# A software-pipelined Perceiver layer: key steps moved a period ahead, the shared unit moved behind the tiles

## What is computed

```python
x = x + xattn(layernorm(x), ctx)     # 16 heads of 128, q and k RMS-normed per head; softmax over 257; @ Wo
x = x + attn(layernorm(x))           # 16 heads of 16, 4 kv heads, rotary, causal; ternary weights; rms_norm(y) @ Wproj
x = x + ffn(layernorm(x))            # below

probs = softmax(xt @ Wg); eidx = argmax(probs); gate = probs[eidx]     # 2048 tokens, 8 experts, top 1
pos = cumsum(onehot) - 1; keep = pos < 256                             # capacity 256 per expert
out = gate * keep * (silu(xe @ W1[e]) * (xe @ W3[e])) @ W2[e]          # hidden width 352
shared = (silu(xt @ sw1) * (xt @ sw3)) @ sw2                           # every token
return out + shared
```

## Time and profile before

| | |
|---|---|
| median of 3 runs | 1421.3 us (1420.99 to 1423.54) |
| the profiled execution | 1421.9 us, its span 1420.0 |
| mean granted TensorE clock | 0.963 |
| busy, share of the span: PE / DVE / ACT / POOL | 89% / 64% / 62% / 40% |
| instructions | 34911 |
| chain that ended last: PE / DVE / issue / ACT / POOL | 51% / 17% / 10% / 8% / 4% |

### The profile page before, as it was taken

How to read it: one execution, slowest core, us unless ns; L and a number is a source line. 1 busy time by engine, 2 the same in 40 slices (tenths; PEclk the granted TensorE clock), 3 DMA queues, 4 the chain that set the end, 5 groups by cost and what they waited for, 6 DMA issues and landing times.

```text
span 1420.0 us, 34911 instructions
## 1 busy us (share of the span) xinstructions
PE 1268.5 (89%) x10526; PEld 852.0 (60%) x10526; DVE 913.5 (64%) x3312; ACT 886.6 (62%) x3732; POOL 571.5 (40%) x1371
## 2 busy tenths in 40 slices
PE   5877999999999999999999999999999999983596
PEld 2644666666665656566666666665656566661485
DVE  6754767767676767676767767776767676753132
ACT  5455676757585767767676767585767767651132
POOL 1053262625344352525262625344352525244153
PEclk9988999999999999999999999999999999995799
DMA  9020010101010000000010101010000000210251
GB/s 351 16 84 8 13 36 11 34 11 34 8 34 11 24 22 23 22 13 25 11 34 11 34 11 34 12 31 11 25 21 23 22 15 23 111 33 2 72 191 47
DMA packets 36563, 55.18 MB, mean 39 GB/s; under 512 B 6797, under 2 KB 29482, under 8 KB 35601
## 3 DMA queue, kind: packets, MB, share of 16 engines
q1 hardware_dynamic: 32064, 46.53, 10.5%
q0 software_dynamic: 3376, 7.98, 1.7%
q10 hardware_dynamic: 1056, 0.02, 0.0%
HBM read 46.54 MB, written 8.42 MB: 39 GB/s over the span
## 4 chain that ended last, share of the span: by engine, by line
PE 51%; DVE 17%; issue 10%; ACT 8%; POOL 4%; DMA 1%; POOLq 0%; DVEq 0%; ACTq 0%
PE AB L600 27%; PE Db L600 9%; PE Eb L600 7%; DVE kst L1374 3%; PE C L600 3%; DVE rq L1431 2%; PE C L729 2%; PE C L744 2%; POOL prob L1190 2%; ACT prob L1022 2%; ACT AB L954 2%; DVE pT L1563 1%; DVE px L1645 1%; ACT wt_q L946 1%; ACT pxT L1054 1%
## 5 line engine op out<-in xcount | busy, mean ns | idle before, releaser
L954 ACT ACTIVATE AB<-AB 128x128 f32<-128x128 f32 (+1 forms) x1160 | 303.4, 262 | 95.8 <-PE AB L600 92.6
L1145 POOL TENSOR_TENSOR pjunk<-pjunk 128x1 f32<-128x1 f32 x289 | 56.3, 195 | 679.3 <-DVE sinv L1558 384.8
L1374 DVE BATCH_NORM_STATS2 kst<-AB 128x6 f32<-128x256 f32 x512 | 181.8, 417 | 107.3 <-PE AB L600 104.7
L600 PE MATMUL AB<-wk_hi,c_hi 128*128 128x512 f16 x512 | 199.5, 390 | 19.3 <-POOL c_lo L1151 7.4
L954 ACT ACTIVATION_READ_ACCUMULATOR AB<-AB 128x1 f32 (+1 forms) x1160 | 216.1, 186 | 0.0
L600 PE MATMUL AB<-wk_lo,c_hi 128*128 128x512 f16 x512 | 198.2, 387 | 0.0
L600 PE MATMUL AB<-wk_hi,c_lo 128*128 128x512 f16 x512 | 197.6, 386 | 0.0
L1022 ACT ACTIVATE prob<-prob,nbias,rq 128x257 f32<-128x257 f32 x256 | 150.6, 591 | 9.2 <-DVE nbias L1553 9.2
L1190 POOL TENSOR_SCALAR prob<-prob,sinv 128x257 f32<-128x257 f32 x256 | 129.2, 505 | 20.1
L600 PE MATMUL AB<-ctxT,qpT 128*128 128x257 f32 x512 | 123.2, 383 | 11.5 <-ACT pxT L1054 11.5
L600 PEld LDWEIGHTS AB<-wk_hi,c_hi 128*128 128x128 f16 x512 | 50.9, 99 | 101.7 <-issue 29.4
(11 more groups left out here) (282 smaller groups left out, 2868.5 us busy)
## 6 DMA issues: line engine op xcount, KB each, us to landing
ctxT<-in_ctxT SPq DMA_DIRECT2D x64, 128.5 KB, 2.1
ctxn<-in_ctxn SPq DMA_DIRECT2D x64, 128.0 KB, 2.1
xin<-in_x SPq DMA_DIRECT2D x16, 128.0 KB, 2.2
prob<-in_wqT SPq DMA_DIRECT2D x1, 2048.0 KB, 16.5
xres<-in_x SPq DMA_DIRECT2D x16, 128.0 KB, 2.1
expert_rows<-base POOLq DMA_DIRECT2D x1, 2048.0 KB, 9.3
out<-base SPq DMA_DIRECT2D x16, 128.0 KB, 1.7
wq_hi<-in_w SPq DMA_DIRECT2D x2, 768.0 KB, 4.2
```

The costliest lines, as they stand in the source:

```text
L600: return pe.matmul(out, lhsT, rhs, start=start, stop=stop)
L954: ins = nc.scalar.activation(k, k, ACT.Square, accum_out=sums[0:m, h:h + 1])
L1145: own.mark(pool.tensor_tensor(pjunk[:, 0:1], pjunk[:, 1:2], pjunk[:, 1:2], ALU.mult))
L1374: ins = V.bn_stats(stats[:, 0, 2 * half + n], AB[0:m, 2 + half, 2 * D * n:2 * D * (n + 1)])
```

## The change

Six things are changed.

1. **Key steps ahead.** A0 to A3 are the key steps of batches 0 and 1 (formerly K0 to K3) of tile i+2, run in period i, one period before the rest of that tile's front half, with their splits a0, a1 (POOL), and AN, gAN, an for the inverse roots. In the prologue they are added at its end, and the loop's period keeps K4 to K7. There are now 14 loop periods, then FIN (tile 14's back half and tile 15's front half, without the A steps), then LAST, both written out as straight code.
2. **Shared unit behind the periods.** up and dn leave the period. SP stores x2 to out and xn2T to a part of the scratch output (store_halfway). LAST does U0 to U15 and D0 to D15 for all 16 tiles with the last tile's own steps among them; SP loads xn2T and x2 back four tiles deep and stores the sums. The rows of the experts are loaded after D9.
3. **Compact last key.** plast is 128 by 12 for a batch, turned by one matmul, and ACT spreads it over the four groups with four scaled copies.
4. **VectorE.** rq is one multiply by a mask, a matmul rx by a spreading matrix, a multiply and a reduction. The four adds of key heads become one, ysq's reduction two adds, and the norm's last operation and the one-hot compare take a broadcast operand in place of a scalar.
5. **Tags.** Each period, POOL sends the tags of the tile before (tg); LAST has two left.
6. **Order.** The lists are written anew. DVE's loop is unrolled by 7.

```diff
-    "PE": """K0 pt3 K1 X K2 o3 K3 f Q xt1 K4 qkv QP rk0 s0 qk sc rk1 K5 K6 K7 pt0 pv s1 st pr rk2 s2 o0 xt2 rk3
-              lg up s3 pt1 dn pos o1 pt2 o2""".split(),
-    "POOL": """h0 n3 h1 X h2 c0 c1 r0 cl ln1 r1 h3 n0 r2 y r3 ln2 c2 n1 c3 n2 scat""".split(),
+    "PE": """pt3 K4 o3 K5 f X rk0 K6 Q xt1 K7 qkv QP rx s0 qk sc rk1 s1 rk2 A0 pt0 pv rk3 s2 st pr s3 A1 pt1 o0 xt2 lg
+              A2 pos o1 pt2 A3 o2""".split(),
+    "ACT": """tl3 ph3 K4 oh3 K5 X K6 Q rk0 xt1 gRQ K7 qkv gqkv gKN1 QP qk e0 rk1 sc rk2 A0 tl0 ph0 pv rk3 e1 e2 A1 tl1
+              ph1 xt2 oh0 e3 lg A2 oh1 tl2 ph2 A3 oh2 gAN""".split(),
+    "DVE": """dp3 K4 do3 K5 X XL f K6 Q RQ K7 qkv KN1 rq qr rx s0 kn1 sc i0 s1 sm A0 dp0 ys yv s2 i1 s3 pr i2 ln2 A1
+              dp1 do0 lg i3 pos A2 do1 dp2 A3 AN an do2""".split(),
+    "POOL": """n3 h2 h3 tg X r0 ln1 r1 c1 c0 c3 r2 a0 n0 a1 r3 c2 cl y n1 ln2 n2 scat""".split(),
+LAST_ORDER = {
+    "PE": """U0 pt3 U1 o3 f D0 U2 xt1 D1 qkv U3 D2 qk sc U4 D3 pv U5 st pr D4 U6 xt2 lg D5 U7 pos D6 U8 D7 U9 D8 U10 D9
+             U11 D10 U12 D11 U13 D12 U14 D13 U15 D14 D15""".split(),
+    "POOL": """n3 tg ln1 y ln2 scat""".split(),
...
+            def store_halfway(p):
+                sp.wait_ge(drained["E"].sem, drained["E"].at(p, "pr"))
+                sp.dma_start(d["out"][bass.ds(p.tile * P, P), :], x2[:]).then_inc(x2_out.sem, 16)
+                sp.wait_ge(drained["D"].sem, drained["D"].at(p, "xt2"))
+                sp.dma_start(turned_rows[bass.ds(p.tile * P, P), :], xn2T[:].rearrange("p k n -> p (k n)")).then_inc(xn2T_out.sem, 16)
...
+            for n in range(TILES):
+                s = BANK_PAIRS[n][1]
+                sp.wait_ge(filled[s].sem, filled[s].at(LAST, f"U{n}"))
+                if n + 4 < TILES - 1:
+                    load_turned(n + 4)
+                sp.wait_ge(drained["E"].sem, drained["E"].at(LAST, f"D{n}"))
+                sp.dma_start(d["out"][n * P:(n + 1) * P, :], back_of(n)).then_inc(sum_out[n % 4] if n < TILES - 1 else last_out, 16)
+                if n + 4 < TILES - 1:
+                    sp.wait_ge(sum_out[n % 4], 16 * (n // 4 + 1))
+                    load_back(n + 4)
+                if n == 9:
+                    load_rows()
...
-                for g in range(G):
-                    ins = mm(Db[0:LK, P * g:P * (g + 1)], plast[:, b, g], ident16[:])
-                ins.then_inc(filled["D"].sem, 1)
+                mm(Db[0:LK, 0:P], plast[:, b], ident16[:]).then_inc(filled["D"].sem, 1)
...
+                for g in range(G):
+                    ins = nc.scalar.activation(pTl[0:LK, b % 2, P * g:P * (g + 1)], Db[0:LK, 0:P], ACT.Copy,
+                                               scale=own_group[0:LK, g:g + 1])
...
+            def step_rx(p):
+                pe.wait_ge(rqt_ready.sem, rqt_ready.at(p, 0))
+                start(p, "rx")
+                mm(Db[:, 0:NB * H], spread32[:], rqm[:].rearrange("p n m -> p (n m)")).then_inc(filled["D"].sem, 1)
...
-                for b in range(NB):
-                    for m in range(4):
-                        src = rqt[SQ * b:SQ * (b + 1)].rearrange("p (g m) -> p g m", m=4)[:, :, m]
-                        ins = V.tensor_scalar(rq[SQ * m:SQ * (m + 1), G * b:G * (b + 1)], src, 1.0 / WQK_SCALE, None, ALU.mult)
...
-                V.tensor_scalar(out, x, mv[:, 0:1], rstd[:, n:n + 1], ALU.subtract, ALU.mult).then_inc(xn_ready.sem, 1)
+                V.scalar_tensor_tensor(out, x, mv[:, 0:1], rstd[:, n:n + 1].broadcast_to([P, DIM]), ALU.subtract, ALU.mult)\
+                    .then_inc(xn_ready.sem, 1)
...
-                    for n in range(TILES - 1):
-                        put_tags(n)
...
-            with loop(pool) as i:
+            with loop(pool) as i:
                 tile(Period("full", i))
+            tile(FIN)
             tile(LAST)
```

More of the change, by code:

```diff
@@ L68, in __init__ @@
         self.kind, self.i = kind, i
-        self.tile = TILES - 1 if kind == "last" else i
-        self.early = 0 if kind == "pro" else i + 1
-KINDS = (("pro", 1), ("full", TILES - 1), ("last", 1), ("expert", E))
+        self.tile = {"fin": TILES - 2, "last": TILES - 1}.get(kind, i)
+        self.early = {"pro": 0, "fin": TILES - 1}.get(kind, i + 1)
+KINDS = (("pro", 1), ("full", TILES - 2), ("fin", 1), ("last", 1), ("expert", E))
 PRO = Period("pro")
 FULL = Period("full")
+FIN = Period("fin")
 LAST = Period("last")
+AHEAD = {"A0", "A1", "A2", "A3", "AN", "gAN", "an", "a0", "a1"}
 class Events:
@@ L83, in __init__ @@
         self.sem, self.unit, self.names = sem, unit, names
+        names.setdefault("fin", [n for n in names.get("full", ()) if n not in AHEAD])
     def before(self, p):
@@ L96, in at, with after @@
         return self.before(p) + (list(self.names[p.kind]).index(name) + 1) * self.unit
+    def after(self, p, name):
+        return self.at(p, name) + self.unit
     def turn(self, p, name):
@@ new lines @@
+LAST_ORDER = {
+    "PE": """U0 pt3 U1 o3 f D0 U2 xt1 D1 qkv U3 D2 qk sc U4 D3 pv U5 st pr D4 U6 xt2 lg D5 U7 pos D6 U8 D7 U9 D8 U10 D9
+             U11 D10 U12 D11 U13 D12 U14 D13 U15 D14 D15""".split(),
+    "ACT": """tl3 ph3 U0 oh3 U1 xt1 U2 qkv gqkv U3 qk sc U4 pv U5 xt2 U6 lg U7 U8 U9 U10 U11 U12 U13 U14 U15""".split(),
+    "DVE": """dp3 U0 do3 f U1 D0 qkv U2 D1 qr U3 D2 sc sm U4 D3 ys yv pr ln2 U5 D4 lg U6 D5 pos U7 D6 U8 D7 U9 D8
+              U10 D9 U11 D10 U12 D11 U13 D12 U14 D13 U15 D14 D15""".split(),
+    "POOL": """n3 tg ln1 y ln2 scat""".split(),
@@ L157 @@
 }
 START_ORDER = {
[L161 to L164, removed]
@@ L165 @@
-    "POOL": """hl h1 h3 h2 h0 rkl X r0 r1 fill cl c0 n0 c1 n1 r2 c2 r3 n2 c3""".split(),
+    "PE": """KL K0 K1 K2 X K3 rkl Q W0 W1 K4 QP rx M01 K5 M23 tw rk0 s0 rk1 s1 K6 pt0 K7 pt1 o0 s2 rk2 A0 rk3 A1 s3 o1 A2 pt2 o2 A3""".split(),
+    "ACT": """KL K0 wq0 K1 wq1 K2 X K3 gKN0 rkl Q W0a W0b W1a W1b K4 gRQ QP M0a M0b K5 M1a M1b tw rk0 e0 rk1 e1 K6 ph0 tl0 K7 gKN1 ph1 tl1 oh0 rk2 e2 A0 rk3 A1 oh1 e3 A2 ph2 tl2 oh2 A3 gAN""".split(),
+    "DVE": """wk low KL KNL K0 K1 X K2 XL wql K3 gg KN0 kn0 Q W0l wt0 W1l K4 RQ rq wt1 rx M01 wt K5 M23 tw s0 s1 i0 K6 dp0 i1 K7 KN1 kn1 do0 dp1 s2 A0 A1 s3 i2 A2 dp2 do1 i3 do2 A3 AN an""".split(),
@@ L166 @@
+    "POOL": """hl h1 h3 h2 h0 rkl X r0 r1 fill cl c0 n0 c1 n1 a0 a1 r2 c2 r3 n2 c3""".split(),
 }
@@ L559, in _ @@
                 early_loads(p)
-            p = Period("full", TILES - 2)
+            p = FIN
             late_loads(p)
@@ L896, in _ @@
                     steps[step](p)
+            for step in steps_of("PE", FIN):
+                steps[step](FIN)
             for step in steps_of("PE", LAST):
@@ L1276, in _ @@
                           f"n{b}": (lambda p, b=b: normalise(p, b)), f"c{b}": (lambda p, b=b: split_rows(p, b))}
+            for b in range(2):
+                steps[f"a{b}"] = lambda p, b=b: split(p, b, ahead=True)
             def tile(p):
```

333 lines of the change are left out of this document (206 added, 127 removed).

## The result

The changed kernel takes 1396.9 us (median of 3, 1392.4 to 1401.2), the ratio to the kernel before is 0.982 [0.980, 0.985]. It is faster, by 24.4 us (1.8%) where 86 were forecast, and above the range's end of 1385. The profiled execution is the slowest of the three, 1401.2 with a span of 1399.4.

The account below looks back on a forecast made before the run. TensorE was taken to bound the periods, a serial chain the last tile. Start +1.6, periods -101.6, FIN and last tile +14.9, experts -1.7 sum to -86.8 us, giving 1335; range 1298 to 1385.

Parts of the forecast that it names:

- all of the old 6.4: Loop period: upper bound of 70.5 us if all 6.4 us read as TensorE waiting stayed beside 64.1 of work.
- The walk: Loop period: steps placed at the later of TensorE's arrival and input's; 4.7 us of waits, 64.1 of work, 68.8 together.
- FIN: Tile 14's period without A steps: 46.1 us of work, 50.8 to 61.2 with waits, taken as 59.
- the last tile: All up and dn steps plus the tile's own: 84.3 us of work and 7 of waits at both ends, 91.
- The compact last key: Loop period: pt's last key as one matmul, 0.32 us becoming 0.08, four times, -0.96 of TensorE work.
- DVE has room: Loop period: DVE loses 16 small scalings, 2.78 us, and other operations; nothing credited beyond the waits named.
- Experts: After the last tile: first up shorter because TensorE is busy before it; -1.7 us, between 0 and -3.0.
- The start: Before the first period's f: ahead key steps come in, others go out, pt2's wait ends later; +1.6 us.
- The clock in the last tile: Forecast: full clock, 84 of 91 us busy. Rival: 1.2 GHz after FIN's waits, +76 us, about 1411, chance 0.06.
- the waits did not shrink to 1.4: Rival, loop period: denser packing leaves 1.4 us of waits, period 65.5, 46 us less, about 1289; chance 0.08.
- Instruction supply: Rival, FIN and LAST: straight code makes TensorE wait for instructions at each sc step; +19 us, about 1354, chance 0.07.
- The circle of dependences: Rival, loop period: the loop from n3 through scat back to n3 keeps the period about 75.7; 1432, chance 0.04.

Follow-up runs that it names:

- c2: The changed kernel with ACT copying the turned probabilities ahead of the four last-key copies in all four batches: 1368.8 us, ratio 0.961.
- c1: The changed kernel with the ahead keys' inverse roots moved behind the first copies of the next period: 1382.6 us, ratio 0.972.
- d1: The changed kernel with three queue-order edits: ahead keys' roots later, turned-probability copies before last-key copies, experts' row loads later: 1353.3 us, ratio 0.953.
- e3: The changed kernel with the three queue-order edits, rq's 16 small scalings back on DVE and no rx: 1403.8 us, ratio 0.986.
- d4: The kernel before with only the tags changed, each tile's sent one period later by one POOL transfer: 1408.7 us, ratio 0.991.
- f1: The changed kernel with the three queue-order edits, and lg, pos and their companions one key step later: 1403.2 us, ratio 0.986.
- d2: The changed kernel with the three queue-order edits and the last key as before, four transposes and one ACT copy: 1355.0 us, ratio 0.954.

## Why the prediction was wrong

**The period, the step that failed.** "I walked the new order with these lengths, each step starting at the later of PE's arrival and its input's" gave 4.7 us of waits, P = 68.8. 72.85 was measured, 57 us more over 14 periods, and above even 70.5, the bound with "all of the old 6.4" as waits. The 4.05 us come in three parts.

The waits were too short by 1.4 us. The walk has 3.95 besides its 0.75 for hand-offs; the table of the change has 74.6 in 14 periods, 5.3 each. The walk took an input's time as its producer's start and duration, without what stands ahead of the producer in its own engine's list. So rk3 and o3 wait 1.3 and 0.7 us for 0.85 and nothing, while pv waits 0.5 for the walk's 1.15. c2 and c1, which only change what stands ahead, take 28 and 14 us off.

The work was too short by 1.9 us. The step lengths of the old period add up to 69.3, and the prediction read the other 6.4 us as waiting. Its own row has TensorE busy 71.61 of 75.66, so 4.05 idle, and the table of waits of the kernel before (139 to 1203) adds up to 51.8 us in 14 periods, 3.7 each. Its first row:

```profile
PE AB L600 <- ACT wt_q L946: 15.8, 14, 1.2
```

So over 2 us of a period were busy time beyond the step lengths, and they stayed in the change: 66.77 busy at full clock, where the sum has 64.1 and 0.75. What they are made of was not looked into.

The granted clock takes the remaining 0.7 us: seven of the change's 14 periods are at 0.96 to 0.98, the others at 1.00 and 72.1 us long.

d1 sets the two larger parts apart. With ACT's list in order its waits are 3.4 us a period, below the walk's, and its period is still 70.3. At full clock it is this row (columns as in the earlier trace rows):

```profile
489.62:559.37 69.75, 66.32 (x593) 44.09 (x591) 48.95 (x181) 52.97 (x240) 34.22 (x83) 1.00 0.08 25
```

What is left over 68.8 are the 1.5 us of busy time that the sum lacked; the shorter waits and the lower clock in five of its periods are 0.6 each and cancel. From FIN's f to the experts d1 takes 149.8 us against my 150, FIN 59.86 for 59 and the last tile 89.95 for 91. So the forecast's terms for these two fit a kernel whose ACT list is in order.

**The compact last key, half priced.** The sum credits TensorE with 0.96 a period, where the one matmul takes 0.15 us (1232.86 to 1233.01) for 0.32, so 0.7, and says nothing of the four copies on ACT, which the earlier trace rows could not show and the diff did. The nearest row, one copy of 12x512 of 0.56 us, would have bounded them at four times that. They cost 2.2 us of ACT a period, and 30 us of time where they stood.

**"DVE has room, so I credit none of it beyond the waits named."** Wrong by 51 us, on d1. A share of 53.1 in 75.66 busy is an average; between the projection of q, k and v and the heads, DVE's new list is the path, as e3 shows.

**The terms that held.** Experts -2.4 for -1.7, the first up at 5.42. The last tile from its first up, at 1229.37, to 1320.61: 91.2 us for 91, with granted clock 1.00. The Trainium skill ("TensorE: Matmul & The Clock Gate", on what is actually happening) says that activity releases the lower clock. The row agrees. That 91 came out so closely is luck:

```profile
1229.37:1320.61 91.24, 81.28 (x740) 73.01 (x738) 40.11 (x109) 32.17 (x71) 3.89 (x6) 1.00 0.28 78
```

It is busy 81.3 where 84.3 were said, and idle 10.0 where 7 were, and most of the idle time lies not at the ends but in the middle, behind the tile's own steps.

**Two that did not.** FIN, from 1163.02 to that up: 66.4 for 59, of which c2 gives 6.4 back. The start: +4.2 for +1.6; in d1 it is -0.6 (138.31 for 138.91).

**The rivals.** None is what happened. The clock in the last tile is 1.00, and the waits did not shrink to 1.4. Instruction supply falls: LAST's sc step took 1.25 us in the change's chain (1259.62). My weighing of the earlier trace rows against the Trainium skill ("Runtime: NRT & Kernel Launch", on instruction fetch mechanics) went the wrong way, d4 shows: the stall had another cause, and nothing here speaks against that page any more. The circle of dependences I put at "some 46 us" by adding durations; by f1 it was within 2.6 us of binding. The sum left out the time for which each member waits for its turn on a busy engine. It did not set the change's period, but it was far nearer than 0.04 of a chance tells.

**Open.** Which of the three DVE edits besides rq matters, and the shared unit's move by itself, were not run. That the key steps ahead are worth anything apart from the order of the lists is not shown.

## What to carry over

When work is taken off the bound engine and another engine gets more pieces for it, price the pieces there, and look up what stands behind them in that engine's list: 0.55 us more at the wrong place four times a period cost 2. Before a rest is called waiting, compare it with the idle time that the trace shows. A walk along one engine's steps is only as good as the other engines' queues in it; a busy share of 70% says nothing of a short serial stretch. The chain of waits names the last releaser, and the idle time on the bound engine's own timeline says what it cost.

## What was not expected of the hardware

The same steps, behind the same wait, can run at full clock in one period and below it in the next. In one of f1's longer periods TensorE's timeline behind sc, and the stretch's granted clock (the last number but two), are:

```profile
462.48 1.28 PE L672 MATMUL AB<-wt_q 16*32 16x32 f32 x128 [1.12 <-ACT wt_q L1030]
463.72 1.57 PE L801 MATMUL C<-consts_sb,rkx 128*128 128x128 f32 x8
465.08 3.12 PE L672 MATMUL AB<-ctxT,qpT 128*128 128x257 f32 x8
```

```profile
457.00:461.00 4.00, 4.00 (x44) 3.74 (x42) 3.62 (x16) 1.38 (x4) 0.00 (x0) 1.00 0.00 0
...
465.00:469.00 4.00, 4.00 (x19) 3.38 (x18) 2.71 (x12) 1.60 (x4) 2.85 (x7) 0.68 0.01 2
```

In one of its shorter periods, where the granted clock stays at 1.00:

```profile
686.46 1.28 PE L672 MATMUL AB<-wt_q 16*32 16x32 f32 x128 [1.12 <-ACT wt_q L1030]
687.70 1.06 PE L801 MATMUL C<-consts_sb,rkx 128*128 128x128 f32 x8
688.60 1.90 PE L672 MATMUL AB<-ctxT,qpT 128*128 128x257 f32 x8
```

Before the fall TensorE was busy but for those 1.12 us from the period's f on. At 0.68 a part of the stretch is at 1.2 GHz and the rest at 2.4; rk1 is 1.57 us long for 1.06, s1 3.12 for 1.90. f1's periods are 72.3, 73.7 or 75.1 long, at 1.00, 0.98 and 0.95. The longer period above has a second fall, to 0.84 and 0.73 in the two stretches of 4 us from 498.91, at the new wait for plast; so one fall costs some 1.4 us. The kernel before has two lengths as well, with 1.00 over a period of 75.67 and 0.98 over one of 77.0. In d2 all 14 lie between 69.85 and 70.40, at 1.00, though sc waits 1.1 us there too. So that wait alone does not bring the fall, and what does was not found. It is a part of why e3 and f1 lose more than they wait: their tables of waits grow by 1.8 and 2.0 us a period over d1's, their periods by 3.2 and 3.7.
